# Sending 86 of 100 small scatters between the row gathers instead of behind them

## The chip, the core and the metric

The kernel runs on one core of one Trainium2 chip. The metric is the device time of one execution in microseconds (us). Names in the profile: PE is TensorE, with PEld its weight loads; DVE is VectorE, ACT is ScalarE, POOL is GpSimd, SP is SyncE.

## The reference

A graph of 12500 nodes of 256 features, with 212500 edges sorted by destination, goes through one layer with three branches. All is float32.

```python
xn = layernorm(x)
x = x + gnn(xn, src, dst) + mix(xn)
x = x + ffn(layernorm(x))

# gnn: mean over incoming edges, then a linear layer with normed rows
agg = segment_sum(xn[src], dst, 12500) / max(deg, 1)
g = concat([xn, agg]) @ weight;  gnn = g / norm(g) + bias
# mix: linear attention, 8 heads of 64: q (k^T v) / n, then Wout
# ffn: a router by graph attention over 131072 other edges chooses 2 of 4 experts
h = x2 @ W_gat;  a_src, a_dst = (h * att_src).sum(-1), (h * att_dst).sum(-1)
e = leaky_relu(a_src[src] + a_dst[dst])        # per edge, softmax per destination
scores = layernorm(segment_sum(softmax(e) * h[src], dst))
ffn = sum over the top 2 experts of gate * (gelu(x2 @ W1 + b1) @ W2 + b2)
```

The term `a_dst` of a node is the "destination term" of the title: four numbers a node, which the router's edges need in the order of their destinations.

## The kernel before

The nodes are cut into 100 node tiles of 125 (`NT`, `NP`). The kernel has three stages that matter here, each a block of programs for the five engines. A block ends with a barrier: no engine starts the next block before all, GpSimd among them, are through with theirs.

The first stage, until 130 us in the trace, loads and norms the rows and stores them as `xn_rows`.

The second stage is the one that is changed. It is a pipeline of steps s = 0, 1, 2 and so on up to 218, and each engine but GpSimd walks the steps with its own list of works, each with a lag (`walk`). In step s, TensorE sums half tile s of the 208 half tiles of edges (`NS`): GpSimd has gathered 8 x 128 rows of `xn_rows` for it into a ring of four half tiles (`rows`), VectorE has made one-hot matrices, and eight matmuls (line 1093) add them into sums by destination node. VectorE also sorts the router's 131072 edges in the first steps, and in step 132 (`PLACES_AT`) finds the places in the sorted order at which each node's run of edges starts and ends (`start_i`, `end_i`).

From step 112 (`POST_AT`) on, node tiles go through a second chain beside the sums, one a step: load of the finished sums, mean, linear layers, residual, second norm, and the router's product, whose result VectorE copies in `router_row` (lines 933 to 936). For node tile t this copy stands in VectorE's step 118 + t. It puts the destination terms into `ad_all[:, t, :]` and adds one to the semaphore `s_hc`. The last node tile's copy is in step 217, ten steps after the last half tile of sums.

GpSimd's program is written out in full and runs in order. For each half tile s it waits until TensorE has summed half tile s - 4, which frees the place in the ring, and sends eight indirect DMAs, one for every 128 rows (line 788). When all 208 half tiles are sent, it sends 100 scatters, one a node tile (line 793): each waits for its copy (`s_hc` at t + 2) and writes 128 rows of four numbers to `ad_rows`, at the place at which the node's edges start:

```python
for t in range(NT):
    pool.wait_ge(s_hc, t + 2)
    pool.indirect_dma_start(out=ad_rows, ...ap=start_i[:, t:t + 1]..., in_=ad_all[:, t, :]).then_inc(s_ads, 16)
```

The third stage loads `ad_rows` after all 100 scatters have landed (`s_ads`). TensorE runs the four experts for all node tiles (lines 1678 and 1686: 16 and 32 matmuls a node tile), while GpSimd gathers the router's rows in 16 batches of 64 indirect DMAs (line 1357) and VectorE works out the attention; the scores of the last batch have their place at node tile 93 of 100. Behind the experts a last part weighs and adds the experts' results.

Of the kernel before, what the change touches and what calls it, by code (L numbers as in the profile page):

```python
# [13 lines left out]
NT = N // NP  # L14
# [41 lines left out]
POST_AT = 2 * SPANS + 4 - NT  # L56
SPANS_AT = SPANS - NT // 2
PLACES_AT = HISTS + 4
LN_TILES = -(-N // P)
LB = 14  # L60
LN_BATCHES = LN_TILES // LB
LN_RING = 4
# [3 lines left out]
LN_SCALED = (0, 2, 1, 5, 6)  # L66
LN_LEFT = N - (LN_TILES - 1) * P

# [88 lines left out]
def build(nc, x, src, dst, gnn_w, gnn_b, wqkv, wkv_t, wout_t, bout, w_gat, att_src, att_dst,  # L157
          b_gat, ln_g, ln_b, w1, b1, w2, b2, fedge, out):
    ctx = ExitStack()
    with ctx:  # L160
# [9 lines left out]
        ad_rows = dram("ad_rows", [AD_ROWS, RH])  # L170
# [29 lines left out]
        start_i = sb("start_i", [P, NT], i32)  # L200
        end_i = sb("end_i", [P, NT], i32)
        small = sb("small", [P, 64])
        ad_all = sb("ad_all", [P, NT, RH])
# [7 lines left out]
        s_ads = sem("s_ads")  # L211
# [30 lines left out]
        junk = lambda j: PS[2 + j // 2][:, j % 2 * D:(j % 2 + 1) * D]  # L242
        nm, vs, sd, rs = (setup.enter_context(nc.sbuf_tensor(n, [P, LN_TILES], f32)) for n in ("nm", "vs", "sd", "rs"))
        ln_st = setup.enter_context(nc.sbuf_tensor("ln_st", [P, LB, 6], f32))
# [44 lines left out]
        with nc.Block() as block:  # L289
# [107 lines left out]
            def _(dve):  # L397
# [6 lines left out]
                def copy_out(first, last):  # L404
                    for k in range(first, last):
                        _, to, n = turned[k]
                        dve.wait_ge(s_tr, k + 1)
                        v.tensor_copy(to, PS[k % 2][:, 0:n * P]).then_inc(s_trc, 1)
# [123 lines left out]
            @block.tensor  # L532
            def _(pe):
                pe.wait_ge(s_const, 2)
                pe.wait_ge(s_gf, 1)
                for k, (of, _, n) in enumerate(turned):
                    if k >= 2:
                        pe.wait_ge(s_trc, k - 1)
                    for q in range(n):
                        last = nc.tensor.transpose(PS[k % 2][:, q * P:(q + 1) * P], of[:, q, :], ident)  # L540
                    last.then_inc(s_tr, 1)
# [82 lines left out]
        with ExitStack() as stage, nc.Block() as block:  # L624
# [66 lines left out]
            s_hc = ev("s_hc")  # L691
# [12 lines left out]
            def _(sp):  # L704
# [9 lines left out]
                def load(j, _, u, w):  # L714
                    sp.wait_ge(s_turn, j + 1)
                    sp.dma_start(x_n[u][:], xn_rows[bass.ds(j * NP, NP), :]).then_inc(s_xl[u], 16)
# [63 lines left out]
            @block.gpsimd  # L780
            def _(pool):
                nc.gpsimd.iota(spare[:], [[1, NP]], base=EF, channel_multiplier=NP, allow_small_or_imprecise_dtypes=True).then_inc(s_sp, 1)

                for s in range(NS):
                    g, h, w = s // 2, s % 2, s // 2 % 2
                    pool.wait_ge(s_used[h], g + 1)
                    for q in range(HU):
                        pool.indirect_dma_start(out=rows[w][h][:, q, 0:D], out_offset=None, in_=xn_rows,  # L788
                                                in_offset=bass.IndirectOffsetOnAxis(ap=gsrc[:, s * HU + q:s * HU + q + 1], axis=0)
                                                ).then_inc(s_rows[w][(h * HU + q) // QUAD], 16)  # L790
                for t in range(NT):
                    pool.wait_ge(s_hc, t + 2)
                    pool.indirect_dma_start(out=ad_rows, out_offset=bass.IndirectOffsetOnAxis(ap=start_i[:, t:t + 1], axis=0),
                                            in_=ad_all[:, t, :], in_offset=None).then_inc(s_ads, 16)

            @block.vector
            def _(dve):
# [202 lines left out]
                def lanes(_, t, u, w):  # L1000
# [13 lines left out]
                    (POST_AT + 3, 0, NT, second_norm), (2, 0, NT, spread),  # L1014
                    (MIX_AT, 0, 1, mixed), (PLACES_AT, 0, 1, places),
                    (SORTED_AT, 0, 1, sorted_ids), (SORTED_AT + 1, 0, 1, same_node), (SORTED_AT + 2, 0, 1, lanes),
# [58 lines left out]
            def _(pe):  # L1075
# [109 lines left out]
                def sort_turn(s):  # L1185
                    _, k, trip, _ = SORT[s]

                    def emit(_, t, u, w):
                        pe.wait_ge(s_go, trip + 1)
                        for r, (lo, hi) in enumerate(TURN_BLOCKS):  # L1190
                            if r:
                                pe.wait_ge(s_tc, 3 * trip + r)
                            for q in range(lo, hi):
                                last = nc.tensor.transpose(TR[:, (q - lo) * P:(q - lo + 1) * P], keys[k % 2][:, q * P:(q + 1) * P], ident)
                            last.then_inc(s_ps, 1)
                    return emit

                def lane_before(_, t, u, w):
# [5 lines left out]
                    (POST_AT + 1, 0, NT, turn_mean), (POST_AT + 4, 0, NT, turn_x2), (POST_AT + 5, 0, NT, router), (0, 0, HISTS, count_nodes),  # L1204
                    (MIX_AT, 0, 1, mixed), (PLACES_AT, 0, 1, places), (SORTED_AT + 1, 0, 1, lane_before), (0, 0, NS, sums)]
                     + [(s, 0, 1, sort_turn(s)) for s in range(SORTED_AT) if SORT[s][0] == "turn"])
# [529 lines left out]
```

## Time and profile before

| | us |
|---|---|
| median of 3 runs | 4270.76 |
| the runs | 4270.12, 4270.76, 4277.53 |
| span of the profiled execution | 5331.2 |
| second stage in it, first gather to last scatter's start | 130.1 to 2820.7 |

The profiled execution's own time beside its span is not shown in what there is; the span is the time from its first to its last instruction. It is 1060 us longer than the median of the runs, which were not recorded.

In the profile, L788 is line 788 of the kernel. A row of the timeline ends with the engine's idle time before the instruction and what ended it: "issue" means nothing that the profile shows, "remote" something that it could not name. A group x100 has 100 instructions. PEclk is the granted TensorE clock as a share of full speed, and the DMA share is the mean busy share of the core's 16 DMA engines.

### The profile page before, as it was taken

The numbers are of one execution on the slowest core, as the hardware profiler recorded it, in microseconds if no ns is written. First come the engines' busy times: TensorE is split into PE (matmuls) and PEld (weight loads), VectorE is DVE, ScalarE is ACT, GpSimd is POOL, SyncE is SP. The second block draws the span as 40 slices with busy tenths as digits, with TensorE's granted clock in tenths as the row PEclk, the third lists the DMA queues.
The fourth block names the chain that finished last, engine by engine and source line by source line (L and its number), as shares of the span: only waits on it lengthen the run. The fifth ranks groups of instructions, "written<-read, shape, count | busy, mean of one in ns | idle before, by whom it ended". The sixth has DMA issues, their size and how long they took to land. (4 is left out here: it accounts for less than half of the span.)

```text
span 5331.2 us, 46344 instructions
## 1 busy us (share of the span) xinstructions
PE 3564.3 (67%) x12937; PEld 2313.0 (43%) x12938; DVE 2082.9 (39%) x4892; ACT 801.1 (15%) x1970; POOL 2832.6 (53%) x2937
## 2 busy tenths in 40 slices
PE   0688888888757777777626377768685777789200
PEld 0455555555445455555413154444453454455100
DVE  5456655665546555544311020211111120212378
ACT  5111211111101111111101011111111111112000
POOL 2666666666666666666655623653636444630420
PEclk9889899998878888888767588888787788899655
DMA  7444444444445555555512111211112111211387
GB/s 250 128 109 115 112 111 112 112 115 112 112 111 148 138 153 154 162 152 152 125 33 61 18 49 28 58 38 48 35 50 43 44 48 36 60 50 48 118 254 253
DMA packets 381413, 540.57 MB, mean 101 GB/s; under 512 B 120314, under 2 KB 297818, under 8 KB 381143
## 3 DMA queue, kind: packets, MB, share of 16 engines
q0 software_dynamic: 119136, 234.44, 20.0%
q1 hardware_dynamic: 243119, 288.12, 16.8%
q10 hardware_dynamic: 19016, 16.48, 0.9%
q8 instruction: 45, 0.74, 0.1%
q14 instruction: 97, 0.79, 0.0%
HBM read 392.03 MB, written 146.74 MB: 101 GB/s over the span
## 5 line engine op out<-in xcount | busy, mean ns | idle before, releaser
L788 POOL DMA_INDIRECT rows<-xn_rows,gsrc x1664 | 1606.6, 965 | 908.5 <-issue 459.8
L1357 POOL DMA_INDIRECT nb<-route_rows,idx x1024 | 1000.3, 977 | 897.7 <-DVE msg L1432 480.9
L1093 PE MATMUL PS<-rows,oh 128*128 128x257 f32 x3328 | 910.0, 427 | 351.9 <-issue 220.0
L1686 PE MATMUL PS<-arena,hid 128*125 128x256 f32 x3200 | 865.1, 422 | 408.5 <-issue 298.6
L1686 PEld LDWEIGHTS PS<-arena,hid 128*125 128x125 f32 x3200 | 662.9, 209 | 621.3 <-issue 502.6
L1093 PEld LDWEIGHTS PS<-rows,oh 128*128 128x128 f32 x3328 | 693.8, 214 | 488.8 <-issue 296.6
L1621 DVE TENSOR_TENSOR y_sb<-PS,b_b 125x512 f32<-125x512 f32 x200 | 128.7, 685 | 1781.4 <-remote 975.2
L1678 PE MATMUL PS<-x2g,arena 128*128 128x500 f32 x1600 | 722.6, 610 | 147.3 <-issue 94.0
L1678 PEld LDWEIGHTS PS<-x2g,arena 128*128 128x128 f32 x1600 | 313.5, 197 | 541.6 <-issue 473.0
L1647 ACT ACTIVATE hid<-PS,b_sb 128x500 f32<-128x500 f32 x400 | 269.9, 677 | 1109.9 <-PE PS L1678 688.9
L1165 PE MATMUL PS<-own_w,p_t 128*125 128x512 f32 x400 | 231.2, 662 | 77.7 <-ACT s_t L1053 54.5
L829 DVE TENSOR_TENSOR oh<-PS,rel 128x1024 f32<-128x1024 f32 x208 | 254.0, 1221 | 9.2 <-issue 1.0
L842 DVE TENSOR_REDUCE ss<-sq 125x16 f32<-125x1024 f32 x100 | 121.7, 1217 | 281.9 <-ACT sq L1043 186.6
L1110 PE MATMUL PS<-arena,x_t 128*125 128x512 f32 x400 | 227.8, 697 | 4.9 <-issue 4.9
L1112 PE MATMUL PS<-arena,x_t 128*125 128x512 f32 x400 | 192.2, 603 | 0.0
L859 DVE TENSOR_TENSOR oh_hi<-PS,arena 128x400 bf16<-128x400 f32 x256 | 144.5, 564 | 78.1 <-remote 63.6
L1037 ACT ACTIVATE kept<-PS 128x257 f32<-128x257 f32 x104 | 40.2, 386 | 892.9 <-remote 686.4
L859 DVE TENSOR_TENSOR oh_lo<-PS,arena 128x500 bf16<-128x500 f32 x256 | 171.3, 669 | 0.0
L1128 PE MATMUL PS<-oh_lo,oh_hi 128*100 128x125 bf16 x1024 | 101.6, 232 | 100.8 <-issue 58.8
L1607 DVE SCALAR_TENSOR_TENSOR acc<-arena,gate,acc 125x256 f32<-125x256 f32 x300 | 145.3, 484 | 40.6 <-issue 19.4
L1373 POOL DMA_INDIRECT res<-rec_rows,end_i x100 | 96.3, 963 | 117.9 <-DVE q L1541 86.8
L1042 ACT ACTIVATE sq<-PS 125x512 f32<-125x512 f32 x100 | 59.7, 597 | 637.9 <-PE PS L1112 328.0
(304 smaller groups left out, 3086.8 us busy)
## 6 DMA issues: line engine op xcount, KB each, us to landing
y_rows<-y_sb SPq DMA_DIRECT2D x100, 512.0 KB
arena<-y_rows SPq DMA_DIRECT2D x100, 512.0 KB
rows<-xn_rows,gsrc POOLq DMA_INDIRECT x1664
nb<-route_rows,idx POOLq DMA_INDIRECT x1024
sum_rows<-kept SPq DMA_DIRECT2D x104, 128.5 KB
x_rows<-x SPq DMA_DIRECT2D x100, 128.0 KB
hid<-x_rows SPq DMA_DIRECT2D x100, 128.0 KB
m_in<-sum_rows SPq DMA_DIRECT2D x100, 125.5 KB
```

What stands on the lines that cost most here:

```text
L788: pool.indirect_dma_start(out=rows[w][h][:, q, 0:D], out_offset=None, in_=xn_rows, in_offset=bass.IndirectOffsetOnAxis(ap=gsrc[:, s * HU + ...
L829: v.tensor_tensor(oh[w][h][:], NUMBERS.rearrange("p (o n) -> p o n", o=1).broadcast_to([P, HU, P]), along(rel[h][:], P), ALU.is_equal).the ...
L859: last = v.tensor_tensor(to[:, 4 * h:4 * h + 4, :], NUMBERS[:, 0:n].rearrange("p (o n) -> p o n", o=1).broadcast_to([P, 4, n]), along(of[: ...
L1093: last = mm(SUM[:, 0:D + 1], oh[w][h][:, q, :], rows[w][h][:, q, :], start=h == 0 and q == 0, stop=h == 1 and q == HU - 1)
L1110: mm(KP[0:NP, :], x_t[u][:, k * NP:(k + 1) * NP], wkv[:, k, 0:INNER], start=k == 0, stop=k == 1)
L1112: last = mm(VP[u][0:NP, :], x_t[u][:, k * NP:(k + 1) * NP], wkv[:, k, INNER:2 * INNER], start=k == 0, stop=k == 1)
L1165: both = lambda k: mm(GM[u][0:NP, :], p_t[q][:, k * NP:(k + 1) * NP], own_w[:, k, :], start=k == 0, stop=k == 1)
L1357: pool.indirect_dma_start(out=nb[b % NBUF][:, c, :], out_offset=None, in_=route_rows, in_offset=bass.IndirectOffsetOnAxis(ap=idx[:, b * W ...
L1607: last = v.scalar_tensor_tensor(out=acc[t % AR][:], in0=y_in[q][0:NP, e * D:(e + 1) * D], scalar=gate[:, t, e:e + 1], in1=acc[t % AR][:] i ...
L1647: a(hid[:, c, :], HP[c % 4][:, 0:4 * NP], ACT.Gelu, bias=b1_sb[:, c:c + 1]).then_inc(s_hid, 1)
L1678: last = mm(HP[c % 4][:, 0:4 * NP], w1_sb[:, k, e, (c % 4) * P:(c % 4 + 1) * P], x2g[u][:, k, :, :].rearrange("p j n -> p (j n)"), start=k ...
L1686: last = mm(Y[j % 2][e // 2][0:NP, (e % 2) * D:(e % 2 + 1) * D], hid[:, 4 * e + k, j * NP:(j + 1) * NP], w2_sb[:, e, k, :], start=k == 0, ...
```

## The change

GpSimd's loop over the half tiles now also sends scatters. From half tile 140 on (`SCATTERS_AT`, eight after the places are found), up to two scatters go behind each eight gathers, as long as the next scatter's node tile is at most s - 122 (`POST_AT` is 112). So half tiles 140 to 157 send two each, 158 to 207 one each: 86 in all. The other 14 stay behind the last gather. A scatter's wait and its data are as before. Nothing else differs.

```diff
+SCATTERS_AT = PLACES_AT + 8
...
+                def scatter(t):
+                    pool.wait_ge(s_hc, t + 2)
+                    pool.indirect_dma_start(out=ad_rows, out_offset=bass.IndirectOffsetOnAxis(ap=start_i[:, t:t + 1], axis=0),
+                                            in_=ad_all[:, t, :], in_offset=None).then_inc(s_ads, 16)
+
+                scattered = 0
                 for s in range(NS):
...
-                for t in range(NT):
-                    pool.wait_ge(s_hc, t + 2)
-                    pool.indirect_dma_start(out=ad_rows, out_offset=bass.IndirectOffsetOnAxis(ap=start_i[:, t:t + 1], axis=0),
-                                            in_=ad_all[:, t, :], in_offset=None).then_inc(s_ads, 16)
+                    for _ in range(2):
+                        if s >= SCATTERS_AT and scattered <= s - POST_AT - 10:
+                            scatter(scattered)
+                            scattered += 1
+                for t in range(scattered, NT):
+                    scatter(t)
```

## Rows read from the trace of the kernel before

**Rows 1.** The page: span, and busy us (share) xinstructions by engine.
```profile
span 5331.2 us, 46344 instructions
...
PE 3564.3 (67%) x12937; PEld 2313.0 (43%) x12938; DVE 2082.9 (39%) x4892; ACT 801.1 (15%) x1970; POOL 2832.6 (53%) x2937
```

**Rows 2.** Busy time by stretch; the first line names the columns.
```profile
core 0: us, PE busy (x) PEld busy (x) DVE busy (x) ACT busy (x) POOL busy (x), PEclk, DMA share, GB/s
1838.70:2642.20 803.50, 591.23 (x2262) 419.40 (x2261) 388.06 (x1201) 108.03 (x442) 522.46 (x544) 0.85 0.58 152
2642.20:2755.50 113.30, 18.06 (x51) 11.28 (x50) 5.77 (x20) 2.87 (x11) 86.22 (x89) 0.58 0.08 11
2755.50:2821.70 66.20, 42.37 (x142) 28.15 (x142) 28.74 (x117) 12.13 (x47) 10.61 (x11) 0.76 0.33 81
4800.00:4900.00 100.00, 95.83 (x352) 65.67 (x350) 34.18 (x92) 21.89 (x30) 0.00 (x0) 1.00 0.14 50
```

**Rows 3.** Timeline of POOL behind the gathers: start, duration, instruction, idle before it.
```profile
2642.43 1.01 POOL L793 DMA_INDIRECT ad_rows<-ad_all,start_i  x1 [0.30 <-issue]
...
2754.51 0.96 POOL L793 DMA_INDIRECT ad_rows<-ad_all,start_i  x1 [0.30 <-issue]
2769.96 0.96 POOL L793 DMA_INDIRECT ad_rows<-ad_all,start_i  x1 [14.48 <-DVE rt L936]
...
2820.69 0.97 POOL L793 DMA_INDIRECT ad_rows<-ad_all,start_i  x1 [0.49 <-issue]
2831.12 0.11 POOL L1342 MEMSET first_e<- 125x16 f32 x1 [9.47 <-POOLq L624]
...
2833.19 0.95 POOL L1357 DMA_INDIRECT nb<-route_rows,idx  x1 [0.30 <-issue]
```

**Rows 4.** Lines 788 and 793: count, min/median/max ns, first and last start.
```profile
L788 POOL DMA_INDIRECT rows<-xn_rows,gsrc x1664: 940/946/1460, 130.1 to 2641.2; - x185
...
L793 POOL DMA_INDIRECT ad_rows<-ad_all,start_i x100: 963/969/1008, 2642.4 to 2820.7; - x100
```

**Rows 5.** The page's costliest groups: busy us, mean ns, idle us before them.
```profile
L788 POOL DMA_INDIRECT rows<-xn_rows,gsrc x1664 | 1606.6, 965 | 908.5 <-issue 459.8
L1357 POOL DMA_INDIRECT nb<-route_rows,idx x1024 | 1000.3, 977 | 897.7 <-DVE msg L1432 480.9
```

**Rows 6.** What POOL waited for over the span: total us, times, longest.
```profile
POOL nb L1357 <- DVE msg L1432: 480.9, 13, 84.2
...
POOL rows L788 <- remote: 259.0, 127, 6.6
...
POOL rows L788 <- PE PS L1095: 142.7, 28, 8.2
...
POOL rows L788 <- PE PS L1093: 46.9, 16, 10.6
```

**Rows 7.** Timeline of PE: its last row.
```profile
4943.85 22.46 PE L1686 MATMUL PS<-arena,hid 128*125 128x256 f32 x96
```

**Rows 8.** POOL's groups from half tile 140 to the last gather.
```profile
L788 POOL DMA_INDIRECT rows<-xn_rows,gsrc x544 | 522.5, 960 | 282.6 <-issue 146.2 <-remote 127.7 <-PE PS L1093 6.7
```

**Rows 9.** Timeline of DVE: the copies that release scatters, and the stall.
```profile
2624.87 0.16 DVE L936 COPY rt<-PS 125x8 f32<-125x8 f32 x1
...
2636.72 0.16 DVE L936 COPY rt<-PS 125x8 f32<-125x8 f32 x1
...
2687.15 0.16 DVE L936 COPY rt<-PS 125x8 f32<-125x8 f32 x1
...
2754.56 0.16 DVE L925 RECIPROCAL rstd<-rstd 125x1 f32<-125x1 f32 x1 [64.88 <-issue]
...
2769.24 0.16 DVE L936 COPY rt<-PS 125x8 f32<-125x8 f32 x1
```

## The prediction

> **What bounds the kernel now.** I read the page first: no engine is busy for more than 67% of the span, and GpSimd for 53% [rows 1], so the bound has to be looked for by stage. The windows over the stage of the change come next [rows 2]. From half tile 140 to the last gather (544 gathers, 68 half tiles, 803.5 us, 11.8 us each) TensorE works 591.23 us, 8.7 us a half tile at a granted 0.85; GpSimd's records cover 522.46 us, but an indirect DMA takes more than its record: from one scatter's start to the next it is (2754.51 - 2642.43) / 88 = 1.274 us [rows 3], of which the record is 0.969 [rows 4]. So GpSimd, with 8 gathers of 1.24 (2066.5 / 1664, below), is the busier of the two at 10 us a half tile; the rest of the 11.8 is one pause before each eight.
>
> Are these pauses there when nothing is recorded? The span is 5331.2 us, the median of the runs 4270.8: the recording adds a quarter, and a sum on the trace alone would mislead. I therefore add up what GpSimd must spend even if it never waits for another engine's compute: 130.1 us to its first gather [rows 4]; the gathers, 1606.6 busy and 908.5 idle less the pauses of 259.0, 142.7 and 46.9 [rows 5, 6], 2066.5; 100 scatters, 127.4; 11.5 to the next stage (9.47 at the barrier, 2 to its first gather) [rows 3]; its 1024 gathers, 1000.3 and 897.7 idle less the 480.9 spent waiting for VectorE [rows 5, 6], 1417.1. The scores of its last batch have their place at node tile 93, so some seven tiles, of 48 matmuls each, are left; at 95.83 / 352 us a matmul [rows 2] they take 91. From the last matmul (4966.3) to the end of the span: 364.9 [rows 7]. Sum 4208 us, and the timed runs take 4271. If an indirect DMA costs the same there, GpSimd sets the pace nearly everywhere, and all its pauses together are at most 62 us, not the 449 of the trace. That is the estimate on which the forecast hangs.
>
> **The change part by part.** Nothing is added to or taken from the 1664 gathers and 100 scatters. 86 scatters move ahead of the last gather: two behind each of the first 18 eights (140 to 157), one behind each of the other 50.
>
> *Cost ahead of the last gather.* 86 x 1.274 = 109.5 us of GpSimd. Of this, x lies in pauses. Bounds of x in the timed runs: 0, and 62 if all that the sum leaves over lay in these 68 half tiles; evenly spread over 208 it would be 20. I take half of that, 10, since other waits have a share in the 62. So the last gather is 99 us later.
>
> Scatters could also take longer beside a working VectorE than alone. Gathers of this stage run beside the same VectorE work and average 960 ns [rows 8], the least is 940 [rows 4]: 20 ns, 2 us over 86, which I leave out. The Trainium skill speaks against the change here: its page "SBUF — State Buffer" (section "SBUF: two separate sides") says that a DMA issued from GpSimd cannot have its descriptors written while VectorE runs an operation in a two-port mode, and gives 620 ns against some 3100. By that each moved scatter could cost 2.5 us more, an estimate of up to 213 us in all; the 960 ns of the trace disagree, and the measurement decides.
>
> *What waits behind it.* The eight gathers that follow stand behind each scatter, and behind them TensorE's sums. The scatter's new wait, for the router row of half tile s - 122, is met: half tile 207 may send rows up to 85, and rows 86 and 87 (counted back from row 89, whose copy released the scatter of 2769.96) were copied at 2624.87 and 2636.72, before the last gather at 2641.2 [rows 3, 4, 9]. Cost 0; if the cover were gone, see the third rival. The scatters' own transfers pass the software queue in front of later gathers: in the stretch that held 88 of them the DMA engines were 0.08 busy, against 0.58 in the gather stage [rows 2]. Spread over 803 us that is 0.01 more: 0. SP's and ScalarE's queues are not passed.
>
> *What goes behind the last gather.* Before: the scatters run one behind the other and the last starts 1.25 + 99 x 1.274 = 127.3 us after the last gather, if the router rows are ready, and then the stage ends. After: 14 are left, 18 us of work, so what ends the stage is the chain that was hidden under the scatters: the router rows themselves. Row 87 is copied 4.5 us before the last gather; rows 88 and 89 need steps that still hold sums, 8.7 us each by TensorE's busy time; rows 89 to 99 took (2820.69 - 2769.96) = 50.7 us for ten steps [rows 3, 9]. -4.5 + 17.4 + 50.7 = 64 us. Bounds: 50, if the ten steps run faster when nothing is recorded, and 75 if the sums of the last two half tiles come one step later.
>
> *Sum for the timed runs.* 99.5 + 64 - 127.3 = +36 us: 4270.8 + 36 = 4307 us. In words: GpSimd's work is the same; before, the router chain lay under the scatters, after it stands alone.
>
> *Sum on the recorded execution.* Its own time beyond the span is not shown, so I go by the span. There the last scatter starts 179.5 us after the last gather, not 127.3, as the other engines nearly stood still during the burst (below). With pauses unchanged: 109.5 + 64 - 179.5 = -6, and up to 18 more if the 14 left stall the others in the same way. Span after: 5325 to 5343, no visible gain or loss.
>
> **The rivals.** *One, the faster side: the gather stage isn't paced by GpSimd in the timed runs either.* Then its pauses are real, one per half tile of (127.7 + 6.7) / 68 = 2.0 us, 1.7 without the usual 0.3 [rows 8], and one scatter of 1.274 fits in. Only the doubled ones stick out, 18 x (2.55 - 1.7) = 15 us. 15 + 64 - 127.3 = -48: 4222 us. It decides from x = 46 us on. For it: TensorE's 8.7 us would be the bound if an unrecorded gather took under 1.09 us. Against it: the 4208 us, which leave no room for such pauses unless GpSimd is cheaper unrecorded.
>
> *Two, also mostly faster: a burst of scatters stops the others in the timed runs as well.* In the 113.3 us of the burst VectorE ran 20 instructions, in the next 66.2 us 117; it stood for 64.88 us and went on at 2754.56, when the burst ended [rows 2, 9]. If that is the chip, breaking up the burst pays: -6 - 10 = -16 us, 4255; with x = 62, 4203; with x = 0, no change. Against it: the same stalling in every burst of gathers would keep the timed runs near the span, which they are not. The Trainium skill, "NOTIFIC — the notification-queue block", section "7.1 Overflow: three behaviours, one of which stalls the engine", says that the block that writes trace records holds its producers back rather than lose a record inside. By it the stall belongs to the recording, and the sum for the timed runs stands; no run here shows that block itself.
>
> *Three, much slower: the new waits aren't met.* GpSimd would stand in front of its gathers until VectorE copies the row, 1 to 2 us in each of 68 half tiles beside the scatter, about +100 more with rings of four half tiles run empty: 4400. Against it: the copies stood ahead of the half tile that needs them in the trace, and a slower GpSimd gives them more time.
>
> *Four, the change does nothing*, because the tail was no bound: excluded on its own, as the barrier waits for GpSimd in either order; it would have to be a balance of x near 46, held in the cases above.
>
> **How the numbers follow.** Forecast as worked out: 0.52; rival one 0.19; rival two 0.25; rival three 0.04. A measurement of this kernel can tell about 0.2%, 8.5 us. Of the forecast's 0.52, 0.48 is slower, 0.03 within (x from 37 up to 55) and 0.01 faster; rival one is faster; rival two is faster with 0.14 and within with 0.11; rival three is slower. Faster 0.34, same 0.14, slower 0.52. The likeliest case's own range is x from 0 to 25 and a tail of 50 to 66: 4278 to 4319. For 8 in 10 the range reaches down through rival two to the price of rival one, where about half of its chance is left out, and not up to rival three: 4220 to 4322.
>
> **What would show it.** In the profile after: scatters between the eights from 1850 us on, 1.27 us each; half tiles of about 13.1 us with one and 14.4 with two; the pause before each eight still near 2 us (recorded, so no proof for the timed runs); the last gather near 2751 us; then 14 scatters waiting for VectorE's row copies, the last some 64 to 80 us after the last gather; no VectorE gap of 64.88 us. If the pauses shrink by what the scatters take, rival one's mechanism is at work even when recorded. If scatters idle on VectorE ahead of half tile 207, it is rival three. The forecast is wrong if the timed median is below 4262 us; then either GpSimd has slack when unrecorded, or the burst does stop the others, and a kernel with the scatters taken out, timed, tells which.

## The result, and the profile after

The changed kernel takes 4312.44 us (median of 4 runs, 4311.60 to 4314.74), the kernel before 4270.44 beside it: a ratio of 1.0095, 95% interval 1.0081 to 1.0109. It is 42 us slower; 36 were forecast.

The profile after is not stretched: its span is as long as its timed runs. First the page (span, busy us and share, the two groups that answer to [rows 5]).

```profile
span 4309.8 us, 46345 instructions
...
PE 3267.2 (76%) x12938; PEld 2186.5 (51%) x12938; DVE 2090.5 (49%) x4892; ACT 805.5 (19%) x1970; POOL 2863.8 (66%) x2937
...
L795 POOL DMA_INDIRECT rows<-xn_rows,gsrc x1664 | 1618.0, 972 | 509.5 <-issue 508.9
L1366 POOL DMA_INDIRECT nb<-route_rows,idx x1024 | 1013.4, 990 | 457.9 <-issue 294.7
```

GpSimd's idle time in front of the gathers fell from 908.5 to 509.5 us, which over 1664 gathers is the 0.3 us that stands in front of every one. The waits name the rest: total us, times, longest.

```profile
POOL nb L1366 <- DMA nb<-route_rows,idx: 163.2, 79, 4.1
...
POOL ad_rows L787 <- DVE rt L945: 34.6, 10, 6.8
...
POOL rows L795 <- PE PS L1104: 0.3, 1, 0.3
POOL rows L795 <- PE PS L1102: 0.3, 1, 0.3
```

Where the trace of before had 449 us of pauses [rows 6], GpSimd waits 0.6 us for TensorE, in all 1664 gathers together. Nothing but its own work holds it up until the last gather. The windows from half tile 140 to the last gather, and from there to the last scatter, answer to [rows 2]; below them stand GpSimd's groups in the first of the two (busy us, mean ns of one, idle us before them).

```profile
core 0: us, PE busy (x) PEld busy (x) DVE busy (x) ACT busy (x) POOL busy (x), PEclk, DMA share, GB/s
1564.30:2366.80 802.50, 594.06 (x2262) 407.46 (x2261) 391.01 (x1202) 111.13 (x442) 610.90 (x629) 0.87 0.60 154
2366.80:2417.30 50.50, 35.14 (x140) 23.93 (x138) 24.56 (x103) 11.26 (x45) 14.53 (x15) 0.86 0.43 96
```

```profile
L795 POOL DMA_INDIRECT rows<-xn_rows,gsrc x544 | 524.7, 965 | 165.7 <-issue 165.7
L787 POOL DMA_INDIRECT ad_rows<-ad_all,start_i x85 | 86.2, 1014 | 25.9 <-issue 25.6 <-DVE rt L945 0.3
```

85 of the 86 moved scatters stand ahead of the last gather; the last, behind the last eight, follows it. The 85 take 86.2 us and 25.9 us in front of them: 112.1 us, 1.32 each, 0.05 more than in the burst of before. No part of it lies in a pause, as there is none. TensorE is busy for 8.7 us a half tile at a granted 0.87, as in the first recording (0.85); the second recording, below, has 8.2 at 0.92. As GpSimd does not wait for it, this is no part of the 42 us. The timeline of GpSimd (start, duration, idle time before and its end) shows two scatters behind eight gathers, and then what stands behind the last gather at 2365.64.

```profile
1573.10 0.95 POOL L795 DMA_INDIRECT rows<-xn_rows,gsrc  x1 [0.30 <-issue]
1574.35 1.01 POOL L787 DMA_INDIRECT ad_rows<-ad_all,start_i  x1 [0.30 <-issue]
1575.67 0.98 POOL L787 DMA_INDIRECT ad_rows<-ad_all,start_i  x1 [0.30 <-issue]
1576.95 0.98 POOL L795 DMA_INDIRECT rows<-xn_rows,gsrc  x1 [0.30 <-issue]
...
2365.64 0.94 POOL L795 DMA_INDIRECT rows<-xn_rows,gsrc  x1 [0.30 <-issue]
2366.89 1.00 POOL L787 DMA_INDIRECT ad_rows<-ad_all,start_i  x1 [0.30 <-issue]
...
2373.30 0.97 POOL L787 DMA_INDIRECT ad_rows<-ad_all,start_i  x1 [0.30 <-issue]
2381.05 0.97 POOL L787 DMA_INDIRECT ad_rows<-ad_all,start_i  x1 [6.78 <-DVE rt L945]
...
2416.30 0.96 POOL L787 DMA_INDIRECT ad_rows<-ad_all,start_i  x1 [0.54 <-DVE rt L945]
2422.81 0.11 POOL L1351 MEMSET first_e<- 125x16 f32 x1 [5.55 <-POOLq L625]
...
2424.86 0.96 POOL L1366 DMA_INDIRECT nb<-route_rows,idx  x1 [0.30 <-issue]
```

Of the 15 scatters there, six follow at once, the other nine wait for VectorE's row copies, 34 us in all, and the last starts 50.7 us after the last gather. Over two thirds of GpSimd's time there is idle: this is the router chain standing alone. The next stage's first gather follows 8.6 us behind.

### The profile page after: what moved, and what is told of

Read it like the earlier page. It is cut to its first block and busy times, and to the rows that moved or that the text cites. A ratio compares the mean times of both kernels' runs of the same rounds, so it can differ in the third digit from the quotient of the medians.

```text
span 4309.8 us, 46345 instructions
## 1 busy us (share of the span) xinstructions
PE 3267.2 (76%) x12938; PEld 2186.5 (51%) x12938; DVE 2090.5 (49%) x4892; ACT 805.5 (19%) x1970; POOL 2863.8 (66%) x2937
## 5 line engine op out<-in xcount | busy, mean ns | idle before, releaser
L795 POOL DMA_INDIRECT rows<-xn_rows,gsrc x1664 | 1618.0, 972 | 509.5 <-issue 508.9
L1366 POOL DMA_INDIRECT nb<-route_rows,idx x1024 | 1013.4, 990 | 457.9 <-issue 294.7
L1102 PEld LDWEIGHTS PS<-rows,oh 128*128 128x128 f32 x3328 | 664.8, 209 | 506.7 <-DMA rows<-xn_rows,gsrc 370.9
L1695 PE MATMUL PS<-arena,hid 128*125 128x256 f32 x3200 | 707.4, 384 | 77.9 <-DVE y_sb L1630 57.1
L1687 PE MATMUL PS<-x2g,arena 128*128 128x500 f32 x1600 | 682.5, 588 | 55.4 <-ACT hid L1656 35.3
L1695 PEld LDWEIGHTS PS<-arena,hid 128*125 128x125 f32 x3200 | 604.8, 190 | 190.3 <-DVE y_sb L1630 58.7
L1174 PE MATMUL PS<-own_w,p_t 128*125 128x512 f32 x400 | 220.9, 635 | 9.3 <-ACT s_t L1062 9.2
L1119 PE MATMUL PS<-arena,x_t 128*125 128x512 f32 x400 | 194.4, 609 | 0.0
L1121 PE MATMUL PS<-arena,x_t 128*125 128x512 f32 x400 | 188.0, 593 | 0.0
L1066 ACT ACTIVATE gsq<-PS 125x256 f32<-125x256 f32 x100 | 38.3, 383 | 676.4 <-PE PS L1174 676.4
L934 DVE RECIPROCAL rstd<-rstd 125x1 f32<-125x1 f32 x100 | 16.3, 163 | 260.6 <-ACT rstd L1072 260.5
```

What stands on the lines that cost most here:

```text
L1102: last = mm(SUM[:, 0:D + 1], oh[w][h][:, q, :], rows[w][h][:, q, :], start=h == 0 and q == 0, stop=h == 1 and q == HU - 1)
L1119: mm(KP[0:NP, :], x_t[u][:, k * NP:(k + 1) * NP], wkv[:, k, 0:INNER], start=k == 0, stop=k == 1)
L1121: last = mm(VP[u][0:NP, :], x_t[u][:, k * NP:(k + 1) * NP], wkv[:, k, INNER:2 * INNER], start=k == 0, stop=k == 1)
L1174: both = lambda k: mm(GM[u][0:NP, :], p_t[q][:, k * NP:(k + 1) * NP], own_w[:, k, :], start=k == 0, stop=k == 1)
L1366: pool.indirect_dma_start(out=nb[b % NBUF][:, c, :], out_offset=None, in_=route_rows, in_offset=bass.IndirectOffsetOnAxis(ap=idx[:, b * W ...
L1687: last = mm(HP[c % 4][:, 0:4 * NP], w1_sb[:, k, e, (c % 4) * P:(c % 4 + 1) * P], x2g[u][:, k, :, :].rearrange("p j n -> p (j n)"), start=k ...
```

## The experiments

**The kernel before, recorded again.** No edit.

> The kernel before, unchanged, recorded once more. Its recorded span of 5331 us was 1060 us longer than the timed runs, while the changed kernel's was 4310, as long as its timed runs. Pace theory (GpSimd is the pace, the stalls of the first recording belonged to that recording): a recording without the stalls has a span of about 4268 us, half tiles of 10.3 us with no pause before each eight, the last scatter 127 to 130 us after the last gather, and the router row of node tile 99 about 50 to 64 us after the last gather, with no VectorE stall in the burst. Rival (a burst of scatters stops the other engines): even where the span is short, VectorE, TensorE and SP stand still during the burst, row 99 comes some 50 us after the burst's end, and the last scatter is about 180 us after the last gather.

One execution, 4280.7 us, with a span of 4278.9. Its page, its windows (half tile 140 to the last gather, then the burst of 100 scatters, then the third stage's gathers), GpSimd's timeline at both ends of the burst, VectorE's row copies in it, and GpSimd's waits:

```profile
span 4278.9 us, 46344 instructions
```

```profile
core 0: us, PE busy (x) PEld busy (x) DVE busy (x) ACT busy (x) POOL busy (x), PEclk, DMA share, GB/s
1563.00:2252.50 689.50, 559.54 (x2248) 391.24 (x2247) 386.77 (x1198) 111.41 (x439) 523.71 (x544) 0.92 0.67 178
2252.50:2380.40 127.90, 34.98 (x141) 23.69 (x139) 24.77 (x103) 11.07 (x45) 97.64 (x100) 0.65 0.19 40
2392.00:3864.00 1472.00, 1328.84 (x4608) 874.10 (x4608) 318.00 (x765) 309.79 (x431) 1016.18 (x1023) 0.96 0.24 62
```

```profile
2251.31 0.95 POOL L788 DMA_INDIRECT rows<-xn_rows,gsrc  x1 [0.30 <-issue]
...
2379.42 0.97 POOL L793 DMA_INDIRECT ad_rows<-ad_all,start_i  x1 [0.30 <-issue]
2389.86 0.11 POOL L1342 MEMSET first_e<- 125x16 f32 x1 [9.47 <-POOLq L624]
...
2391.93 0.95 POOL L1357 DMA_INDIRECT nb<-route_rows,idx  x1 [0.30 <-issue]
```

```profile
2247.44 0.15 DVE L936 COPY rt<-PS 125x8 f32<-125x8 f32 x1
...
2256.73 0.16 DVE L936 COPY rt<-PS 125x8 f32<-125x8 f32 x1
...
2305.10 0.16 DVE L936 COPY rt<-PS 125x8 f32<-125x8 f32 x1
```

```profile
POOL nb L1357 <- DMA nb<-route_rows,idx: 161.9, 79, 3.9
...
POOL ad_rows L793 <- DVE rt L936: 0.6, 2, 0.3
...
POOL rows L788 <- PE PS L1095: 0.3, 1, 0.3
```

The pauses are gone, and so are the stalls: half tiles take 10.1 us, GpSimd waits 0.3 us for TensorE, and during the burst VectorE copies rows 90 (2256.73) to 99 (2305.10, 53.8 us after the last gather), while the scatters run on to 2379.42, 128.1 us after it. The scatters cover the router chain wholly; they wait 0.6 us for it. Rival two falls: a burst of 100 scatters does not stop the other engines. Why the first recording had the stalls was not tried; this one and those of the six other kernels do not have them.

**43 moved instead of 86.**

```diff
-                    for _ in range(2):
-                        if s >= SCATTERS_AT and scattered <= s - POST_AT - 10:
-                            scatter(scattered)
-                            scattered += 1
+                    if s >= NS - 43:
+                        scatter(scattered)
+                        scattered += 1
```

> 43 of the 100 scatters move, one behind each of the last 43 eights; 57 stay behind the last gather. Pace theory: the stage ends 43 x 1.27 = 55 us of gathers later plus the longer of 57 x 1.28 = 73 us of scatters and the router chain of 51 to 64 us, against 128 before: 55 + 73 - 128 = 0, so 4270 us, the same within 5 us. If the cost were proportional to the scatters moved (a moved scatter costs something of itself, beside hiding nothing): 43 / 86 of +42 = +21, 4291. Rival (a burst stops the others): the burst is 57 instead of 100 long, 55 us less stall, 4215 to 4250.

4272.55 us, ratio to before 1.0003 (0.9994 to 1.0012): no change, and not the 4291 of a cost in proportion to the scatters moved. The last gather and the last scatter in GpSimd's timeline:

```profile
2301.80 0.94 POOL L795 DMA_INDIRECT rows<-xn_rows,gsrc  x1 [0.30 <-issue]
...
2375.72 0.96 POOL L787 DMA_INDIRECT ad_rows<-ad_all,start_i  x1 [0.30 <-issue]
```

The last gather comes 50.5 us later than in the second recording of before, and the tail is 73.9 instead of 128.1 us long. The 58 scatters behind the last gather still cover the chain. Moving a scatter costs nothing of itself that the timing can tell (some 4 us over all 43): it is GpSimd's time spent earlier.

**64 moved.** The same edit with `NS - 64`.

> 64 of the 100 scatters move, one behind each of the last 64 eights; 36 stay, 46 us of work. Pace theory: 64 x 1.27 = 81 us later, then the router chain of 51 to 64 us stands alone: 81 + 51 to 64 - 128 = +4 to +17, 4274 to 4287. Proportional cost: 64 / 86 of +42 = +31, 4301. Rival (a burst stops the others): below 4250.

4282.08 us, ratio 1.0026 (1.0016 to 1.0037): +10 against the kernel before beside it (4272.01), inside the 4274 to 4287 that were expected and below the 4301 of a proportional cost. GpSimd's timeline: the last gather, the last scatter that follows at once, the first that waits, the last of all.

```profile
2331.94 0.94 POOL L795 DMA_INDIRECT rows<-xn_rows,gsrc  x1 [0.30 <-issue]
...
2372.90 0.97 POOL L787 DMA_INDIRECT ad_rows<-ad_all,start_i  x1 [0.30 <-issue]
2377.49 0.97 POOL L787 DMA_INDIRECT ad_rows<-ad_all,start_i  x1 [3.62 <-DVE rt L944]
...
2388.27 0.97 POOL L787 DMA_INDIRECT ad_rows<-ad_all,start_i  x1 [0.54 <-DVE rt L944]
```

The 37 scatters behind the last gather run out before the chain does, and the last five wait for row copies. The tail is 56.3 us. The knee lies between: with 58 behind the last gather nothing is lost, with 37 some ten us, with 15 some forty.

**The 86 left out.** This kernel leaves out the 86 scatters that moved, so the destination terms of node tiles 0 to 85 are missing.

```diff
                         if s >= SCATTERS_AT and scattered <= s - POST_AT - 10:
-                            scatter(scattered)
                             scattered += 1
...
-                sp.wait_ge(s_ads, 16 * NT)
+                sp.wait_ge(s_ads, 16 * 14)
```

> The changed kernel with the 86 moved scatters left out, and the load of the destination terms waiting for the 14 that stay: the destination terms of node tiles 0 to 85 are missing. Pace theory: GpSimd's gathers go on 86 x 1.27 = 109 us earlier, the chain behind the last gather is as in the changed kernel: 4312 - 109 = 4203 us, 67 below the kernel before. If GpSimd isn't the pace and the moved scatters lie partly in pauses, less comes back: with pauses of 0.6 us a half tile some 68 us, 4244; if the 42 us arise behind the gathers, under 40 us, above 4270.

4195.01 us, ratio to before 0.9822 (0.9809 to 0.9836). Against the changed kernel, each by its ratio to the kernel before, it is (1.0095 - 0.9822) x 4271 = 117 us less, 1.36 for each of 86, and 8 below the 4203 that were expected. GpSimd's timeline: the last gather, the first scatter that waits, the last scatter, and the end of the barrier behind it.

```profile
2248.92 0.95 POOL L795 DMA_INDIRECT rows<-xn_rows,gsrc  x1 [0.30 <-issue]
...
2265.39 0.97 POOL L787 DMA_INDIRECT ad_rows<-ad_all,start_i  x1 [9.11 <-DVE rt L944]
...
2304.48 0.97 POOL L787 DMA_INDIRECT ad_rows<-ad_all,start_i  x1 [0.54 <-DVE rt L944]
2313.44 0.11 POOL L1350 MEMSET first_e<- 125x16 f32 x1 [8.00 <-POOLq L625]
```

The last gather stands at 2248.92, 116.7 us ahead of that of the changed kernel, and the tail is 55.6 us, as the chain alone makes it. All that the moved scatters take comes back at the last gather when they go: their time was on the path in full. The whole gain is not theirs alone: the tail is 4.9 us longer than in the changed kernel, so the last scatter comes 111.8 us earlier, and what follows it took 8 us less by the two spans (4309.8 and 4189.6), for which no run here shows a cause.

**Only 50 scatters, all behind.** This kernel leaves out the first 50, so the destination terms of node tiles 0 to 49 are missing.

```diff
-                for t in range(NT):
+                for t in range(NT - 50, NT):
...
-                sp.wait_ge(s_ads, 16 * NT)
+                sp.wait_ge(s_ads, 16 * 50)
```

> The kernel before with only the last 50 scatters, all behind the last gather, and the load waiting for 50: the destination terms of node tiles 0 to 49 are missing. Pace theory with a router chain of 51 to 54 us: the 50 scatters take 64 us and still end last, so 64 us go: 4207 us, row 99 is copied some 54 us after the last gather and the last scatter does not wait for it. With a chain of 64 us or more, as first predicted, the scatters would have to wait for the last copies. Rival (a burst stops the others): up to 115 us go, below 4170.

4207.64 us, ratio 0.9853 (0.9838 to 0.9868) to a kernel before of 4267.92: 60 to 63 us less, where 64 were expected. GpSimd's last gather and last scatter, and VectorE's last row copy:

```profile
2252.76 0.95 POOL L788 DMA_INDIRECT rows<-xn_rows,gsrc  x1 [0.30 <-issue]
...
2316.66 0.97 POOL L793 DMA_INDIRECT ad_rows<-ad_all,start_i  x1 [0.30 <-issue]
```

```profile
2309.04 0.15 DVE L936 COPY rt<-PS 125x8 f32<-125x8 f32 x1
```

Row 99 is copied 56.3 us after the last gather, 7.6 us ahead of the last scatter, which does not wait. So 50 scatters cover the chain with 7.6 us to spare, and the chain is shorter than the 64 us of the forecast.

**Fewer waits in the third stage.** If GpSimd paces the third stage too, the waits that its program makes there by itself are on the path.

```diff
-REST = 16
+REST = 64
```

> The kernel before with one constant changed: in the third stage GpSimd waits for all gathers sent so far every 64 gathers instead of every 16. Pace theory (GpSimd's own time sets the pace of the third stage too): in the undisturbed recording 79 waits for landings there cost 162 us, some 2 us each; 48 of them go, about 98 us, but TensorE is busy for 1329 of the 1472 us, so at most some 120 can come back: 4175 to 4200 us. Rival (bursts of indirect DMAs hold the other engines up, which the short waits relieve): longer bursts cost TensorE what GpSimd gains: 4260 or slower.

4167.26 us, ratio 0.9757 (0.9738 to 0.9776): 101 us below the median of the kernel before beside it (4267.92), 8 us below the 4175 to 4200 that were expected, and faster than both kernels of this case. GpSimd's waits for its own landings, and the stretch of the third stage's gathers:

```profile
POOL nb L1357 <- DMA nb<-route_rows,idx: 48.1, 32, 4.8
```

```profile
core 0: us, PE busy (x) PEld busy (x) DVE busy (x) ACT busy (x) POOL busy (x), PEclk, DMA share, GB/s
2388.00:3752.00 1364.00, 1317.66 (x4608) 869.41 (x4608) 317.76 (x765) 310.43 (x431) 1013.92 (x1023) 0.99 0.25 67
```

162 us of waits became 48: 47 of the 79 went, as expected, and the 32 that are left take 1.5 us each instead of 2. The gathers take 1364 us instead of 1472; TensorE is now busy for 1318 of them at a granted 0.99, so little is left there. The rival fails again: longer bursts did not slow TensorE.

## Why the prediction was right

By its steps, against the second recording of before; the two recordings are 4309.8 and 4278.9 long.

- *Who paces.* The sum of GpSimd's own time, 4208 us, said that at most 62 us of pauses were left in the timed runs. In the gathers they are 0.3 us. The first recording's pauses were no property of the timed runs, and the sum found that from the stretched trace alone. Rival one, which needed them, falls.
- *Cost ahead of the last gather.* The forecast was 99.5, with x = 10 in pauses; the last gather went from 2251.31 to 2365.64, which is +114.3. There are no pauses for x, so half the even share was 10 us too much; a scatter beside the gathers took 1.32 instead of 1.274, 4 us over all; and one scatter too many was counted, 1 us the other way. The 2 us that are left are within what the gathers alone differ by: the second recording, the kernel without the 86 and the one with 50 send the same up to the last gather, which stands at 2251.31, 2248.92 and 2252.76.
- *VectorE beside the scatters.* A moved scatter's record took 1014 ns on the mean beside VectorE's work, where [rows 8] has 960 for gathers; in the burst it took 969 (86.22 / 89, [rows 2]). These are the 4 us of the step before; the forecast had put them at 2 and left them out. By the prediction's estimate from the Trainium skill's "SBUF — State Buffer", section "SBUF: two separate sides", up to 213 us could have come; the trace disagrees with that size here.
- *The new waits.* In the gather stage the moved scatters idle 0.3 us on row copies: the cost is 0, as forecast, and rival three falls.
- *The tail before.* 127.3 us were forecast and 128.1 measured.
- *The tail after.* 64 us were forecast and 50.7 measured. The term that was mis-sized is the lag of the row copies. The forecast counted from the stretched trace, in which row 87 was the last before the last gather, and put two more steps with sums, rows 88 and 89, 17.4 us, in front of the ten steps from row 89 to row 99. In all seven other recordings row 89 is copied before the last gather. VectorE's copies of rows 89 and 99 in the changed kernel:

```profile
2359.26 0.15 DVE L945 COPY rt<-PS 125x8 f32<-125x8 f32 x1
...
2415.86 0.15 DVE L945 COPY rt<-PS 125x8 f32<-125x8 f32 x1
```

  So both of these steps were already done: row 89 comes 6.4 us ahead of the last gather, not 13 behind it, which is 19 us earlier than forecast. From there to the last scatter's start it takes 57.0 us instead of 50.7, 6 us more, for which no run shows a cause. It is not the sums: sixteen matmuls, those of the last two half tiles, follow row 89 in the first recording (copy at 2769.24 [rows 9]) as they do in the changed kernel. TensorE's rows, first recording and changed kernel:

```profile
2770.37 6.49 PE L1093 MATMUL PS<-rows,oh 128*128 128x257 f32 x16
```

```profile
2369.05 3.73 PE L1102 MATMUL PS<-rows,oh 128*128 128x257 f32 x16
```

- *Left out.* The way from the last scatter to the third stage's first gather fell from 12.5 to 8.6 us, and the third stage's gathers took 2 less. 114.3 + 50.7 - 128.1 - 3.9 - 2.2 = +31, the difference of the two spans. The timed difference is 42: the second recording's own run, 4280.7, lies 9 above the median of before (4272.01) beside it.
- *Sum.* +36 us were forecast and +42 measured. The mechanism was right, but that the number came so near is in part luck: the two errors, 15 too little ahead of the last gather and 13 too much behind it, nearly cancel.
- *The recorded execution.* The forecast was 5325 to 5343, and 4309.8 was measured. That sum took the stalls as lasting, which they weren't, and so the signs that were named for that trace, pauses of near 2 us and a last gather near 2751, did not come either.

## What to carry to other kernels

When one engine sets the pace and its queue never waits, moving its work earlier gains nothing in itself: count what runs under that work where it stands, for it will stand alone afterwards. Here scatters could move ahead freely only as long as those left behind still covered the 51 to 56 us of the router chain. And when a trace is much longer than the timed runs, add up what each engine must spend without waiting: if one sum comes near the timed runs, as here, that engine is likely the pace, whatever pauses the trace shows.

## What was not expected of the hardware

Two recordings of one kernel differed by a quarter (spans 5331.2 and 4278.9). In the longer one TensorE was busy for 18.06 us and VectorE for 5.77 of the 113.3 us in which GpSimd sent 89 scatters one behind the other [rows 2]; the cause stays open.

The barrier behind the second stage held GpSimd for 9.47 us in both recordings of the kernel before, for 5.55 in the changed kernel and for 8.00 in the one without the 86, whose last scatters are spaced like those of the changed kernel. They are spaced in the first recording of before too [rows 3]. So a burst right in front of the barrier is not what makes the difference, and what does is not shown.
